# Filler matmuls on TensorE in the additive attention loop of a four-layer graph network, and loads of counts in another order

## The reference

```
projected = (x @ W).reshape(N, HEADS, OUT_CH)          # 4 heads of 32
src = projected[row]
dst = projected[col]
scores = jnp.tanh(src + dst)
scores = jnp.einsum('ehc,hc->eh', scores, att)
scores = jnp.exp(scores - jnp.max(scores, axis=0, keepdims=True))
out = jax.ops.segment_sum(src * scores[:, :, None], col, num_segments=N)
normalizer = jax.ops.segment_sum(scores, col, num_segments=N)
out = out / jnp.maximum(normalizer, 1e-12)[:, :, None]
```

## Time and profile before

| | |
|---|---|
| median of three executions | 4942.16 us |
| the profiled execution, first to last instruction (span) | 4898.1 us |
| between the two (start and end of the program) | 44.1 us |
| PE busy | 3999.0 us, 82% |
| DVE busy | 2847.4 us, 58% |
| ACT busy | 1737.4 us, 35% |
| POOL busy | 2828.1 us, 58% |
| mean granted TensorE clock | 0.852 |
| additive loop (gathers, L2172 and L2109 in it) | about 680 to 1915 us |
| second convolution's sum | from about 453 us |

### The profile page before, as it was taken

One profiled execution on the slowest core, in us unless ns is written; L12 is line 12 of the kernel. 1 busy time (PEld: TensorE's weight loads), 2 busy tenths in 40 slices (PEclk: granted clock), 3 DMA queues, 4 the chain that ended last, 5 costly groups with the idle time before them and its releaser, 6 DMA issues. The chain is left out here.

```text
span 4898.1 us, 89702 instructions
## 1 busy us (share of the span) xinstructions
PE 3999.0 (82%) x22566; PEld 2260.3 (46%) x22566; DVE 2847.4 (58%) x8457; ACT 1737.4 (35%) x4474; POOL 2828.1 (58%) x3060
## 2 busy tenths in 40 slices
PE   3997927788887877488888888885399999999987
PEld 1344414445544544344444444442256655556652
DVE  7994032333333334555555555556678888888868
ACT  3773023344344334333333333331322222222227
POOL 0122356666666663555555555554368888888862
PEclk8998957776777777688988888886699999999999
DMA  2333422222222221333333333330056666666650
GB/s 80 91 87 103 147 71 57 57 56 57 57 56 57 56 57 27 113 98 96 97 97 96 96 97 96 97 96 18 21 97 104 105 105 104 104 105 104 104 110 13
DMA packets 377425, 402.41 MB, mean 82 GB/s; under 512 B 86457, under 2 KB 322502, under 8 KB 377030
## 3 DMA queue, kind: packets, MB, share of 16 engines
q0 software_dynamic: 151904, 198.72, 21.0%
q1 hardware_dynamic: 225382, 202.21, 14.4%
HBM read 312.91 MB, written 87.78 MB: 82 GB/s over the span
## 5 line engine op out<-in xcount | busy, mean ns | idle before, releaser
L897 POOL DMA_INDIRECT gathered<-table,sources x952 | 903.6, 949 | 600.6 <-issue 259.9
L1709 POOL DMA_INDIRECT sums<-gathered,idx x606 | 988.7, 1632 | 217.8 <-issue 166.4
L1571 PE MATMUL bank<-wide 128*128 128x512 bf16 x3636 | 851.5, 379 | 0.0
L2228 DVE TENSOR_REDUCE neg_raw<-bank 80x1 f32<-80x512 f32 (+1 forms) x404 | 276.6, 685 | 725.9 <-remote 252.1
L897 POOL DMA_INDIRECT wide<-table,sources x464 | 438.7, 946 | 275.1 <-issue 125.7
L1571 PEld LDWEIGHTS bank<-wide 128*128 128x128 bf16 x3636 | 347.7, 98 | 364.1 <-issue 1.7
L2178 ACT ACTIVATE msg<-bank,neg_top 80x512 f32<-80x512 f32 (+1 forms) x404 | 275.7, 682 | 643.1 <-DVE neg_top L2230 353.6
L1222 POOL TENSOR_TENSOR acc<-acc,msg 128x20 f32 x404 | 108.3, 268 | 411.2 <-issue 244.6
L2221 DVE TENSOR_TENSOR zact<-zact,bank 128x512 f32<-128x512 f32 x404 | 259.5, 683 | 123.1 <-ACT zact L2170 72.9
L2106 PE MATMUL bank<-zact,att_cells 128*32 128x512 f32 x808 | 289.4, 732 | 37.9 <-issue 36.2
L2088 PEld LDWEIGHTS bank<-ident,gathered 128*128 128x128 f32 x1360 | 191.8, 165 | 258.0 <-issue 232.2
(11 more groups left out here) (406 smaller groups left out, 7603.9 us busy)
## 6 DMA issues: line engine op xcount, KB each, us to landing
zact<-in_src_flat SPq DMA_DIRECT2D x202, 192.0 KB
edge_rows<-in_attr_rows SPq DMA_DIRECT2D x202, 128.0 KB
dst_pair<-local_rows SPq DMA_DIRECT2D x177, 128.0 KB
gathered<-table,sources POOLq DMA_INDIRECT x952
dst_pair<-local_rows SPq DMA_DIRECT2D x202, 64.0 KB
counts<-wide SPq DMA_DIRECT2D x4, 3000.0 KB
counts<-fm_ab SPq DMA_DIRECT2D x4, 3000.0 KB
fm_ab<-counts SPq DMA_DIRECT2D x4, 3000.0 KB, 11.0
```

Of the source, the lines that this page charges most:

```text
L897: pool.indirect_dma_start(out=g[:, j, :], out_offset=None, in_=table, in_offset=bass.IndirectOffsetOnAxis(ap=mine, axis=0)).then_inc(rows_ ...
L1571: pe.matmul(k.bank[b][:, :], k.split[t.two][:, c, :], k.source_hot[t.two][:, b * CHUNK:(b + 1) * CHUNK], start=first, stop=c == PARTS - 1, ...
L1709: pool.indirect_dma_start(out=k.sums[j], out_offset=bass.IndirectOffsetOnAxis(ap=k.idx[t.slot][:, j:j + 1], axis=0), in_=out_rows(t)[:, j, ...
L2228: dve.tensor_reduce(raw, score_bank(t), AX.X, ALU.max, negate=True).then_inc(top_found, 1)
```

## The change

Two edits.

In the additive loop, `sums` on PE waits first for `kept` of tile t-2 (so that its bank is free), then updates the semaphore `turns_begun`, then runs WARM1 = 4 matmuls that nobody reads: 128 x 128 fp16 weights and 432 columns, both from the table `iota_c`, written to the columns 80 to 511 of the bank whose first 80 columns take the tile's sums. Only then does it wait for `weight_ready`. In the GAT loop only the order of the two waits is changed.

In `sum_counted`, the waits on a value computed from a register are gone for the thirds 1 to 3 of the first group. Two thirds are loaded in the rebuilding loop as before. The third one is loaded once, behind the loop, so behind the store of the rebuilt tile and behind the landing of the second third. PE waits for the first third in its own rebuilding loop, for a semaphore `second_there` that SP sets, and for the third third's landing. `rounds_done` is updated and waited for by nobody.

```diff
--- before.py
+++ after.py
@@ -59,6 +59,7 @@
 HEADS2 = 2
 STRIDE1 = WIN
 STRIDE2 = 32
+WARM1 = 4
 
 
 def ceil_div(a, b):
@@ -1354,6 +1355,7 @@
             hot_ready, counted, evicted, stored, free = (st.sem("hot_ready"), st.sem("counted"), st.sem("evicted"),
                                                          st.sem("stored"), st.sem("free"))
             loaded, begun = [st.sem(f"loaded{i}") for i in range(2)], [st.sem(f"begun{i}") for i in range(3)]
+            second_there, rounds_done = st.sem("second_there"), st.sem("rounds_done")
             summed, kept, adds_begun, added = st.sem("summed"), st.sem("kept"), st.sem("adds_begun"), st.sem("added")
             thirds = [(i * GROUP // 3, (i + 1) * GROUP // 3) for i in range(3)]
 
@@ -1367,18 +1369,26 @@
                 @block.sync
                 def _(sp):
                     sp.sem_inc(free, 1)
-                    for landed in begun:
+                    for landed in begun[0:2]:
                         sp.sem_inc(landed, 16)
+
+                    def load_third(i):
+                        lo, hi = thirds[i]
+                        sp.dma_start(k.counts[0][:, lo:hi, :], k.all_counts[lo:hi, :, :].rearrange(
+                            "t p c -> p t c")).then_inc(begun[i], 16)
                     with sp.Fori(0, k.rebuild) as n:
-                        for (lo, hi), landed in zip(thirds, begun):
-                            sp.wait_ge(landed, n * 16 + 16)
-                            sp.dma_start(k.counts[0][:, lo:hi, :], k.all_counts[lo:hi, :, :].rearrange(
-                                "t p c -> p t c")).then_inc(landed, 16)
+                        for i in range(2):
+                            sp.wait_ge(begun[i], n * 16 + 16)
+                            load_third(i)
                         sp.wait_ge(evicted, n + 1)
                         sp.dma_start(k.all_counts[bass.ds(tile(n), 1), :, :].rearrange("t p c -> (t p) c"),
                                      again).then_inc(stored, 16)
                         sp.wait_ge(stored, n * 16 + 16)
                         sp.sem_inc(free, 1)
+                        sp.wait_ge(begun[1], n * 16 + 32)
+                        sp.sem_inc(rounds_done, 1)
+                    sp.sem_inc(second_there, 1)
+                    load_third(2)
 
                     def load(now):
                         if now is None:
@@ -1409,6 +1419,7 @@
                     with pe.Fori(0, k.rebuild) as n:
                         pe.wait_ge(hot_ready, n + 1)
                         cell_counts(k, pe, 0, k.bank[0]).then_inc(counted, 1)
+                        pe.wait_ge(begun[0], n * 16 + 32)
 
                     def sums(now):
                         if now is None:
@@ -1416,8 +1427,10 @@
                         pe.wait_ge(loaded[now.par], (now.pair + 1) * 16)
                         wait_count(pe, kept, now.g - 1)
                         for i, (lo, hi) in enumerate(thirds if first(now) else [(0, now.size)]):
-                            if first(now):
-                                pe.wait_ge(begun[i], k.rebuild * 16 + 16)
+                            if first(now) and i == 1:
+                                pe.wait_ge(second_there, 1)
+                            if first(now) and i == 2:
+                                pe.wait_ge(begun[2], 16)
                             for b in range(k.blocks):
                                 mm = block_sums(k, pe, parts, now, b, lo, hi)
                         mm.then_inc(summed, 1)
@@ -2128,9 +2141,18 @@
                     pe.matmul(top_bank(t), a.own[lanes(t), :], k.top_cells[lanes(t), :], start=True,
                               stop=True).then_inc(top_turned, 1)
 
+                def keep_warm(bank, free, count):
+
+                    for _ in range(count):
+                        pe.matmul(bank[:, free:CHUNK], k.iota_c[:, 0:P], k.iota_c[:, 0:CHUNK - free], start=True,
+                                  stop=True)
+
                 def sums(t):
+                    wait_count(pe, copied if gat else kept, t.t if gat else t.t - 1)
+                    if not gat:
+                        pe.sem_inc(turns_begun, 1)
+                        keep_warm(k.bank[6 + t.two], cells, WARM1)
                     pe.wait_ge(weight_ready, t.t + 1)
-                    wait_count(pe, copied if gat else kept, t.t if gat else t.t - 1)
                     if merge:
                         merge.finish_spreads(pe, t)
                     g = rows(t)
```

## The result

Nineteen executions each: before 4942.38 us median, now 4949.05 us. The ratio is 1.0013, 95% interval [1.0007, 1.0019]: 6.7 us slower, where 8 us faster was forecast. The time lies in the stated range and within the 0.2% called no change, but its sign is clear and it is the other one.

What follows compares the result with a forecast made beforehand. It took POOL's gathers and stops, not PE's clock, to bound the additive loop. -6 there and -1.5 in the second GCN stage took 4898.1 to 4890.6 us; with 44.1 us kept, forecast 4934 us, range 4905 to 4965.

Steps and rivals of the forecast that it cites:

- POOL's account: Additive loop: 1002 us of gathers with issue plus 229 us in 96 stops, 1231 us, make up its 1235 us.
- the change can gain or lose only by what it does to these stops: Additive loop: only POOL's 96 stops, 229 us of waits between runs of gathers, could carry a gain or loss.
- The fillers' length and the clock: Additive loop on PE: fillers take 145 to 291 us in all; mean clock rises from 0.73 to 0.85.
- That is covered with 3.9 us over: Additive loop: at full clock two tiles with fillers take 8.3 us, within a 12.2 us piece of eight gathers.
- half of them going is -6 us: Additive loop: five of ten four-gather pieces vanish, each saving 1.2 us, -6 us.
- my ten of the profile before: Additive loop: ten pieces of four gathers counted, most at half clock, each costing 1.2 us extra.
- Rival 3: Additive loop: fillers hold back sums, a quarter of fifty-one pieces lose 3.3 us, 4984 us; four pieces, 4954; together 18%.
- Rival 2: Additive loop: faster PE makes longer runs, three tiles in 18.1 us instead of two in 12.2, the rule; 4915 us, 20%.
- Rival 1: Additive loop: PE's clock binds; full clock removes the stops, -229 us, 4712 us; chance 5% for anything of the kind.
- The second GCN stage: Third load behind the store: PE's first sums start near 462.8, 2.3 us earlier; -1.5 us taken.
- I keep that: Whole kernel: the 44.1 us between profiled span and median, taken as program start and end, was kept.
- the sum: Whole kernel: -6 - 1.5 = -7.5 us on the profiled 4898.1, plus the 44.1 us; forecast 4934 us.

Runs made afterwards that it cites:

- e7: Changed kernel without fillers and without the `far` matmul in the additive loop (output differs): 0.9972 of before, on a chip where before takes 4909.7 us.
- e1: Changed kernel with no filler matmuls (WARM1 = 0), new waits and loads kept: 0.9996 of before, on a chip where before takes 4905.4 us.
- e4: Changed kernel with sixteen fillers a tile instead of four: 1.0212 of before, on a chip where before takes 4905.4 us.
- e2: The changed kernel once more, four fillers a tile: 1.0009 of before, on a chip where before takes 4905.4 us.
- e18: Changed kernel without fillers, attention matmul of the additive loop in fp16: 1.0010 of before, on a chip with stops where before takes 4942.5 us.
- e5: Changed kernel with its four fillers moved to the head of PE's step: 1.0026 of before, on a chip where before takes 4909.7 us.
- e11: Changed kernel without fillers and without any gathers in the additive loop (output differs): 0.9328 of before, on a chip where before takes 4382 us.
- e13: Changed kernel without fillers, on a chip without stops where before takes 4384 us: 0.9999 of before.
- e14: The changed kernel, four fillers, on a chip without stops where before takes 4384 us: 0.9993 of before.
- e3: Changed kernel with eight fillers a tile instead of four: 1.0032 of before, on a chip where before takes 4905.4 us.
- e17: Changed kernel with four fillers and the attention matmul in fp16: 1.0000 of before, on a chip with stops where before takes 4942.5 us.
- e15: Changed kernel without fillers, attention matmul in fp16, on a chip without stops where before takes 4384 us: 1.0090 of before.
- e16: Changed kernel with four fillers and the attention matmul in fp16, on a chip without stops where before takes 4384 us: 0.9976 of before.

## Why the prediction was wrong, step by step

- **POOL's account: right up to the last gather.** There the loop is gathers plus stops in every run with stops. That "the change can gain or lose only by what it does to these stops" is wrong: PE's work behind the last gather lasted 30 us before, 32 in e7, 40 in e1, 66 in e4, and the next layer's first gather follows some 100 us behind its end each time.
- **The fillers' length and the clock: right.** 145 to 291 us were bounded, 214 us measured; 0.85 forecast, 0.84 measured. No row of before shows the 0.85, and by what the fillers raise the clock no run took apart.
- **"That is covered with 3.9 us over" with "half of them going is -6 us": the step that failed.** I set the cover against a piece of two tiles and counted the short pieces. These hardly moved with the fillers (6 without, 7 with four, e1 and e2), and my ten of the profile before were no base for a gain: e1, without fillers and on a chip of the same kind, has 6. The long ones did move, 23 to 15. In place of -6 us stand +8.7 us of stops, 4.0 us of loop and 6.0 us of median. That pieces of 8 didn't follow the clock in the earlier trace rows said nothing on which piece comes up. That whether a third tile is ready by a stop hangs on PE's time, which grew by 45 us net, fits the doses and e7; it is argued, not shown, and e18, with 23 long pieces at 998 us, doesn't fit.
- **Rival 3 had the sign and the mild size, but not the place.** It spoke of pieces that lose 3.3 us. In fact pieces of 8 stayed at 12.2 us (e1, e2); they only became more frequent. e5 speaks against the fillers' place ahead of the sums, since they cost no less at the head of the step, though with a wait of their own there. Rival 2 had the right quantity, the number of long pieces, and the wrong direction.
- **Rival 1: nearly nothing in it with the stops, real without them.** The rule of the Trainium skill, TensorE: Matmul & The Clock Gate, "HAM oscillation — how this bites in real kernels", to keep the engine busy, pays once here: for the fp16 kernel without stops, 1.0090 to 0.9976. By that rule the changed kernel should have won; 0.11 more of clock (e1 to e2) came with 0.13% more time.
- **The second GCN stage: right in mechanism, its size open.** PE began at 462.60 for a forecast 462.8. From the first of the three loads to the first gather of the additive loop it was 215.8 us before, 212.6 in the changed kernel and 212.8 to 214.7 in the nine others of the table: 1 to 3 us for the forecast 1.5, against one profile of before. What runs ahead of this stage varies by 7 us (the first load leaves at 453.7 in e1, at 460.2 in e5), and e1's 0.9996 can't tell the gain from zero.
- **"I keep that", of the 44.1 us: wrong, but harmless** for a difference; it was another chip. (By its own terms the sum gives 4934.7, not 4934.)

Open: what holds PE's signals back while POOL issues gathers, and why on some chips only; and what the rest of the +8.7 us is made of beside the rarer long pieces. No run took that apart. Nothing beats both kernels everywhere: fp16 with four fillers does without stops (0.9976) and is equal with them (1.0000).

## What to carry to other kernels

Fillers aren't free because one engine's share shows idle time: ask what their net busy time (their length less what the clock gives back) does to the event that sets the pace, count how often each outcome of it comes up, not only how long each lasts, and look at what the engine still has to do when the pace-setter is done. Where the clock is already high without them (1.00 in e11), or another engine sets the pace, they gain nothing; where a matmul is made lighter, read the clock afterwards, since busy time can grow. Compare profiles of one chip only.

## What the runs showed of the hardware

- Three kinds of chip run the same program in 4382, 4905 and 4942 us. On the fast kind a PE signal's event comes 0.01 us after it (e13, e14); on the others 3.0 to 3.9 us (medians in the additive loop of before, after, e1, e2, e3, e7, e17 and e18) while POOL issues gathers, and 0.01 us ahead of them (e1). A gather is 0.95 us long on both.
- A PE that is busy 400 of 400 us can stay at 1.2 GHz (e15), with weight loads in 69% of that time beside it; with four more fp16 matmuls a tile among the same work it ran at 0.83 (e16), and with the fp32 attention matmul at 0.84 without any (e13).
